# Counts of a GNN layer built two fifths at a time, heavy with light, and their place read from a four-word row

## The chip, the cores and the metric

The kernel runs on one core of a Trainium2 chip. The metric is the device time of one execution in microseconds (us), as the median of several runs. A change counts as faster or slower against the kernel before on the same chip.

## The reference, cut to what matters

A graph of 12500 nodes and 200000 edges goes through two SAGE layers, a last matrix and a layer norm. Edges come sorted by `dst`, and `dst` is drawn as 12500·u², so low nodes have far more edges than high ones.

```python
dst = (12500 * uniform(200000) ** 2.0).astype(int32)      # then sorted, src with it
def _sage_conv(x, src, dst, W_l, b_l, W_r):
    msgs = x[src]
    agg = segment_sum(msgs, dst, num_segments=N_NODES)
    deg = segment_sum(ones, dst, num_segments=N_NODES)
    mean = agg / maximum(deg, 1.0)[:, None]
    return mean @ W_l + b_l + x @ W_r
h = relu(_sage_conv(x, src, dst, W1_l, b1, W1_r))
h = relu(_sage_conv(h, src, dst, W2_l, b2, W2_r))
out = layernorm(x + (h @ W3 + b3))
```

## The kernel before

**Two ways to sum the messages.** The nodes are cut into 100 ranges of 125. The last 304 groups of 512 edges go the general way, in both layers: GpSimd (POOL in the profile) gathers rows of `x` by `src` into a ring of four groups (L420), VectorE (DVE) writes a one-hot matrix of `dst` (`mark_groups`, L929), TensorE (PE) multiplies the two (`pair`, L507), and DVE adds the product to `acc` (`add_product`, L907). The first 348 blocks of 128 edges belong to the five "hot" ranges, and go another way: a matrix of counts A[src, dst] is built once per hot range and multiplied with all rows of `x` ("dense steps", `dense_step`, L578), again in both layers.

**How counts are built.** A hot range has 25 chunks of five nodes. For each chunk DVE reads a row of a small table (`chunk_row`, L937: first block `hb` and the number of pairs of blocks `more`), marks each pair of blocks (`mark_blocks`, one L968 and two L971 a pair), PE multiplies the marks into the bank `psB` (`count_blocks`, L552), and DVE copies `psB` into `scratch` (`keep_counts`, L1012). The copy of one chunk stands just ahead of the marks of the next. Where it goes, and which store to DRAM must have landed first, DVE works out in registers from the number `kept` of chunks kept so far (L997 to L1009).

**Fifths.** Five chunks make a fifth, and `scratch` has two halves for a fifth each. SyncE (SP in the profile) stores a full half to DRAM (`store_part`, L363, 1250 KB), and the next fifth but one is written to the same half. Before, a fifth is built from its first chunk to its last, in the order third, fourth, fifth, first, second. The chunks of the first fifth of range 0 are the heavy ones, since its nodes have the most edges.

**The order of the work in layer 1.** All engines run the same written-out loop: stage 0 has 48 groups, and builds the counts of range 0. In each of the next four stages of 48 groups the counts of the next range are built while the last 40 groups also carry the 20 dense steps of the range before. A chunk is built after every second group. Then come the dense steps of the last range, and layer 2, in which no counts are built. SP's queue is in program order: for each dense step two loads of rows of `x` and one of counts (L326, L330, L349), which wait until the step two before has been used (L338), and between them the stores of the range under way: after steps 7, 11, 17 and 19 and at the end (`STORE`, L384).

```python
STORE = (7, 11, 17, 19)
turned = np.roll(np.arange(HW * CH).reshape(HW, CH), -2 * PART, axis=1).reshape(-1)   # order of chunks
```

Of the kernel before, what the change touches and what calls it, by code (L numbers as in the profile page):

```python
# [39 lines left out]
HW = 5  # L40
# [21 lines left out]
SW = 2 * (P + CJ)  # L62
STORE = (7, 11, 17, 19)
BANKS = 3
# [11 lines left out]
def hot_end(w):  # L76

    return 4 + STAGE * (w + 1) + STAGE


# [18 lines left out]
def constants():  # L99

    import numpy as np
    c = np.zeros((P, C_N), np.float32)
    c[:, C_ID:C_ID + P] = np.eye(P)
    c[0:WN, C_RES:C_RES + WN] = np.eye(WN)
    c[WN, C_RES:C_RES + WN] = 1
    c[:, C_WT:C_WT + NW] = WN * np.arange(NW)
    turned = np.roll(np.arange(HW * CH).reshape(HW, CH), -2 * PART, axis=1).reshape(-1)
    c[:, C_BS:] = CJ * turned
    order = np.array(ORDER)
    d = np.zeros((HW * CH, D_N), np.float32)  # L110
# [12 lines left out]
    b = np.arange(HB)  # L123
    d[:, D_RB:D_RB + HB] = HB - b
    d[:, D_RB + HB:] = b + 1
    w = np.append(order, 0).astype(np.int32).reshape(1, NW + 1) * RW
    k = np.arange(FN)
    n = np.concatenate([np.arange(CJ), k // (CD * SJ) * CJ + k % (CD * SJ)]).astype(np.int16)
    return c, d, w, n.reshape(1, CJ + FN)
# [10 lines left out]
def build(nc, x, src, dst, W1l, b1, W1r, W2l, b2, W2r, W3, b3, c_f, c_s, c_win, c_node, out):  # L140
# [5 lines left out]
    with ExitStack() as ctx:  # L146
# [35 lines left out]
        tab = tables[0:1, :]  # L182
        tabh = tables[32:33, 0:2 * (NH + NW) + 1]
        win = tables[64:65, 0:NW + 1]
# [100 lines left out]
        def _(sp):  # L285
# [29 lines left out]
            for q in range(2):  # L315
                sp.dma_start(xt[WN:WN + 1, q * D:(q + 1) * D], b3.rearrange("(a n) -> a n", a=1)).then_inc(s_w, 16)
            sp.dma_start(win, c_win).then_inc(s_w, 16)

# [39 lines left out]
            def store_part(w, f):  # L358

                n = w * PARTS + f  # L360
                sp.wait_ge(s_bank, credit[s_bank] + (n + 1) * PART)
                sp.wait_ge(s_kept, credit[s_kept] + 16 * n)
                sp.dma_start(a_dram[w * PARTS + (f + 2) % PARTS], scratch[:, n % 2 * JP * PW:(n % 2 + 1) * JP * PW]).then_inc(s_kept, 16)  # L363

# [61 lines left out]
        def _(pe):  # L426
# [40 lines left out]
            pe.wait_ge(s_ring1, 1)  # L467
            pe.wait_ge(s_w, 16 * 11)
            pe.wait_ge(s_set, 1)
# [13 lines left out]
            def turn_spans():  # L483

                pe.wait_ge(s_span, 1)
                for k, (a, n) in enumerate(((0, NH), (1, NH), (2, NW), (3, NW))):
                    pe.transpose(psT[0:1, k * 128:k * 128 + n], span[0:n, a:a + 1], ident[0:n, 0:n])
                pe.matmul(psT[0:1, 127:128], span[0:NW, 4:5], onec, start=True, stop=True).then_inc(s_spanT, 1)
                pe.wait_ge(s_tabh, 1)
                pe.load([wins], tabh[0:1, 2 * (NH + NW):2 * (NH + NW) + 1])  # L490

# [29 lines left out]

            def chunk_row():
                pe.load([more], tabh[0:1, bass.ds(pe.snap(at_row, min_val=1, max_val=2 * (NH + NW) - 1), 1)])
                pe.reg_add(at_row, at_row, 2)

# [56 lines left out]
            def fallback(l, q):  # L582

                W = RW if l == 0 else D
                pe.reg_mov(at_row, 2 * (NH + HW) + 1)
                end = pe.snap(wins, min_val=1, max_val=NW)
                if q == 0:
                    pe.reg_add(fin_x, fin_x, 32)
                pe.wait_ge(s_fall[q], pe.snap(fin_x, min_val=32, max_val=32 * STEPS))
                with pe.If(HW < end):  # L590
                    with pe.Fori(HW, end):
                        for h in range(2):
                            chunk_row()
# [160 lines left out]
        def _(v):  # L754
# [77 lines left out]
            v.wait_ge(s_set, 1)  # L832
            v.wait_ge(s_w, 16 * 11)
            v.wait_ge(s_k, 16)
# [10 lines left out]
            part, at_a = (v.alloc_register(f"v_{q}") for q in ("part", "at_a"))  # L845
            turned = v.alloc_register("v_turned")
            v.reg_mov(hot, 1)
            for r in (hadd, xdone, fdone, fb, kept):
                v.reg_mov(r, 0)
# [3 lines left out]
            def spans():  # L853

                v.wait_ge(s_limT, 1)
                th = tabh[0:1, 0:2 * (NH + NW)].rearrange("o (n c) -> o n c", c=2)
                for q, n in enumerate((NH, NW)):
# [25 lines left out]
                for q in range(2):  # L883
                    v.tensor_copy(th[:, 0:NH, q], psT[0:1, q * 128:q * 128 + NH])
                    v.tensor_copy(th[:, NH:, q], psT[0:1, (2 + q) * 128:(2 + q) * 128 + NW])
                link(v.tensor_copy(tabh[0:1, 2 * (NH + NW):], psT[0:1, 127:128]))
                v.sem_inc(s_tabh, 1)
                v.load([wins], tabh[0:1, 2 * (NH + NW):2 * (NH + NW) + 1])

# [46 lines left out]
            def chunk_row():  # L936
                v.load([hb, more], tabh[0:1, bass.ds(v.snap(at_row, min_val=0, max_val=2 * (NH + NW) - 2), 2)])  # L937
                v.reg_add(at_row, at_row, 2)
# [56 lines left out]
            def keep_counts():  # L995

                v.reg_alu(part, kept, 205, ALU.mult)  # L997
                v.reg_alu(part, part, 10, ALU.logical_shift_right)
                v.reg_alu(at_a, part, -PART, ALU.mult)
                v.reg_add(at_a, at_a, kept)  # L1000
                v.reg_alu(at_a, at_a, CD * SJ, ALU.mult)
                v.reg_add(kept, kept, 1)
                v.reg_alu(turned, part, 1, ALU.bitwise_and)
                v.reg_alu(turned, turned, JP * PW, ALU.mult)
                v.reg_add(at_a, at_a, turned)
                v.reg_alu(part, part, 16, ALU.mult)
                v.reg_add(part, part, credit[s_kept] - 16)
                at = v.snap(at_a, min_val=0, max_val=JP * PW + (PW - CD) * SJ)
                landed = v.snap(part, min_val=16, max_val=16 * HW * PARTS)  # L1009
# [26 lines left out]
            def fallback(l):  # L1036
                v.reg_mov(at_row, 2 * (NH + HW))
                end = v.snap(wins, min_val=1, max_val=NW)
# [6 lines left out]
                with v.If(HW < end):  # L1045
                    with v.Fori(HW, end) as w:
                        for h in range(2):
                            chunk_row()
                            chunk(FN, fbase[:, 0:1], CJ)
# [50 lines left out]
            def layer(l, dense):  # L1100
# [39 lines left out]
                if l == 0:  # L1140
# [7 lines left out]
                    with v.Fori(0, HW - 1) as w:  # L1148
                        chunk_row()
                        keep_counts()  # L1150
                        hot_chunk()
                        with v.Fori(0, STAGE // 4 - STEPS // 2):
                            four(builds=True)
                        with v.Fori(0, STEPS // 2):
                            four(builds=True, w=w)
                    keep_counts()
                    fallback_start()
# [32 lines left out]
        def _(act):  # L1190
# [26 lines left out]
            act.wait_ge(s_set, 1)  # L1217
            act.wait_ge(s_w, 16 * 11)
            give(act, s_tc, s_h, s_z, s_tc2, s_y, s_sd)
# [126 lines left out]
```

## Time and profile before

| | us |
|---|---|
| median of 3 runs (lowest, highest) | 3304.33 (3302.39, 3308.82) |
| the profiled execution: time, span | 3299.5, 3297.4 |
| busy in the span: PE, POOL, DVE, ACT | 2754.1, 2379.8, 1457.7, 497.5 |
| first and last copy of a chunk (L1012) start at | 72.4, 1374.4 |

The page gives each engine's busy time in the span from the first to the last instruction. A name like DVEq is an engine's queue: the register, branch and load instructions that are not counted as its work but take its time. "issue" is time in which an engine waited for nothing that the profile shows. The chain is the run of work that ended last, followed back from the end; what does not stand on it can grow a little at no cost.

### The profile page before, as it was taken

The numbers are of one execution on the slowest core, as the hardware profiler recorded it, in microseconds if no ns is written. First come the engines' busy times: TensorE is split into PE (matmuls) and PEld (weight loads), VectorE is DVE, ScalarE is ACT, GpSimd is POOL, SyncE is SP. The second block draws the span as 40 slices with busy tenths as digits, with TensorE's granted clock in tenths as the row PEclk, the third lists the DMA queues.
The fourth block names the chain that finished last, engine by engine and source line by source line (L and its number), as shares of the span: only waits on it lengthen the run. The fifth ranks groups of instructions, "written<-read, shape, count | busy, mean of one in ns | idle before, by whom it ended". The sixth has DMA issues, their size and how long they took to land.

```text
span 3297.4 us, 61445 instructions
## 1 busy us (share of the span) xinstructions
PE 2754.1 (84%) x13183; PEld 2294.5 (70%) x13184; DVE 1457.7 (44%) x3301; ACT 497.5 (15%) x1511; POOL 2379.8 (72%) x2439
## 2 busy tenths in 40 slices
PE   4788899899899899888866779878879879988876
PEld 3555687678678688677754567767768767767765
DVE  5676555555555555433323333333333333333332
ACT  2000110101111111111110112112112112212113
POOL 4765777677677677767747777777777777777775
PEclk7989999999999999999988889999999999999999
DMA  4443577577677777877655657757757757757743
GB/s 117 130 134 112 169 237 246 173 231 238 203 219 238 222 218 240 263 217 218 206 180 177 190 174 224 216 172 227 216 162 233 221 169 225 225 168 229 219 128 109
DMA packets 495816, 650.77 MB, mean 197 GB/s; under 512 B 184192, under 2 KB 414454, under 8 KB 492503
## 3 DMA queue, kind: packets, MB, share of 16 engines
q0 software_dynamic: 116736, 318.92, 32.6%
q1 hardware_dynamic: 298164, 253.95, 25.2%
q10 hardware_dynamic: 80800, 76.82, 7.7%
q14 instruction: 98, 0.78, 0.1%
q8 instruction: 18, 0.29, 0.0%
HBM read 579.07 MB, written 70.40 MB: 197 GB/s over the span
## 4 chain that ended last, share of the span: by engine, by line
PE 29%; POOL 24%; issue 18%; DVEq 14%; DMA 7%; DVE 7%; SPq 1%; ACT 1%; ACTq 0%; POOLq 0%; PEld 0%; PEldq 0%
POOL ring L420 24%; PE ps L507 16%; PE ps L578 5%; DMA ring<-z_rows,scol 4%; PE psY L622 3%; DVEq L917 2%; DVE oh L971 2%; PE psY L611 2%; DVEq L937 2%; DVE acc L907 1%; DMA counts<-scratch 1%; DVE oh L929 1%; PE psB L552 1%; DVEq L1067 1%; DVEq L914 1%
## 5 line engine op out<-in xcount | busy, mean ns | idle before, releaser
L507 PE MATMUL ps<-ring,oh 128*125 128x257 f32 (+1 forms) x6384 | 1586.9, 400 | 375.7 <-DMA ring<-z_rows,scol 203.6
L507 PEld LDWEIGHTS ps<-ring,oh 128*125 128x125 f32 x6384 | 1221.7, 196 | 649.5 <-issue 462.4
L420 POOL DMA_INDIRECT ring<-in_x,scol x1216 | 1193.4, 981 | 493.7 <-issue 349.8
L420 POOL DMA_INDIRECT ring<-z_rows,scol x1216 | 1185.8, 975 | 397.7 <-issue 355.5
L929 DVE SCALAR_TENSOR_TENSOR oh<-dcol,cf,iota 128x500 f32<-128x500 int16 x798 | 591.4, 741 | 609.9 <-issue 328.3
L907 DVE TENSOR_TENSOR acc<-ps,acc x802 | 338.8, 422 | 608.0 <-PE ps L507 415.4
L578 PE MATMUL ps<-scratch 128*125 128x257 f32 (+1 forms) x2000 | 481.2, 388 | 19.4 <-issue 13.4
L578 PEld LDWEIGHTS ps<-scratch 128*125 128x125 f32 x2000 | 456.1, 294 | 39.3 <-issue 21.5
L1268 ACT ACTIVATE work<-psT,b2c 128x125 f32<-128x125 f32 x200 | 62.0, 362 | 1196.2 <-PE psT L673 1196.2
L1232 ACT COPY work<-psY 125x256 f32<-125x256 f32 x100 | 37.2, 372 | 1306.1 <-PE psY L611 1306.1
L552 PE MATMUL psB<-oh 128*128 (+1 forms) x546 | 160.2, 391 | 81.7 <-DVE oh L971 80.7
L622 PEld LDWEIGHTS psY<-work,w 128*128 128x128 f32 x1600 | 200.6, 197 | 7.4 <-issue 1.1
L622 PE MATMUL psY<-work,w 128*128 128x125 f32 x1600 | 199.8, 280 | 0.7 <-issue 0.7
L971 DVE TENSOR_SCALAR oh<-iota,cf,key 128x500 int16 (+1 forms) x546 | 199.4, 407 | 0.0
L552 PEld LDWEIGHTS psB<-oh 128*128 (+1 forms) x546 | 50.0, 97 | 173.8 <-issue 145.0
L1012 DVE COPY scratch<-psB 128x500 f32 x125 | 84.9, 679 | 114.0 <-issue 104.2
L611 PE MATMUL psY<-w,hT 128*125 128x256 f32 x400 | 113.5, 409 | 17.7 <-issue 16.0
L669 PE MATMUL psT<-hT,w 128*128 x800 | 121.8, 275 | 0.1
L669 PEld LDWEIGHTS psT<-hT,w 128*128 128x128 f32 x800 | 113.0, 192 | 6.4 <-issue 0.5
L968 DVE TENSOR_TENSOR oh<-iota,key 128x256 int16 (+1 forms) x273 | 114.4, 419 | 6.9 <-PE psB L552 4.5
L655 PE MATMUL psY<-w,work 128*125 128x256 f32 x400 | 106.5, 389 | 3.4 <-ACT work L1268 2.6
L611 PEld LDWEIGHTS psY<-w,hT 128*125 128x125 f32 x400 | 73.2, 196 | 49.7 <-issue 36.7
(120 smaller groups left out, 1100.2 us busy)
## 6 DMA issues: line engine op xcount, KB each, us to landing
scratch<-counts SPq DMA_DIRECT2D x200, 312.5 KB
scratch<-in_x SPq DMA_DIRECT2D x114, 512.0 KB, 4.2
scratch<-z_rows SPq DMA_DIRECT2D x114, 512.0 KB, 4.0
counts<-scratch SPq DMA_DIRECT2D x25, 1250.0 KB
work<-in_x ACTq DMA_DIRECT2D x200, 125.0 KB
ring<-in_x,scol POOLq DMA_INDIRECT x1216
ring<-z_rows,scol POOLq DMA_INDIRECT x1216
scratch<-in_x SPq DMA_DIRECT2D x114, 128.0 KB, 5.2
```

The lines of the kernel that those rows point to most:

```text
L420: pool.indirect_dma_start(ring[:, slot, b, 0:D], None, rows_dram, bass.IndirectOffsetOnAxis(scol[:, n - C0:n - C0 + 1], 0)).then_inc(rows[ ...
L507: mm = pe.matmul(psA[0:WN, bass.ds(bank, W)], oh[:, R if later else slot, b, :], ring[:, slot, b, 0:W], start=(b == 0), stop=(b == nb - 1))
L552: mm = pe.matmul(psB[:, 0:n], oh1[:, bass.ds(at, P)], oh1[:, bass.ds(at + P, n)], start=first and b == 0, stop=True, skip_group_check=True)
L578: mm = pe.matmul(psD[0:WN, 0:W], lin_a[:, q, :, :, k].rearrange("p f n -> p (f n)"), lin_x[:, q, k, 0:W], start=(q == 0 and k == 0), stop= ...
L611: mm = pe.matmul(psZ[0:WN, 0:D], hT[:, k * WN:(k + 1) * WN], w2[:, k, 0:D], start=(k == 0), stop=(k == 1))
L622: mm = pe.matmul(psH[:, m * WN:(m + 1) * WN], w1[:, a, k, m * P:(m + 1) * P], tT[:, 2 * a + k, :], start=(a == 0 and k == 0), stop=(a == 1 ...
L655: pe.matmul(at, tT[:, k, :], w3[:, k, :], start=(k == 0), stop=False)
L669: pe.matmul(psT[:, m * WN:(m + 1) * WN], w2[:, k, D + m * P:D + (m + 1) * P], hT[:, bass.ds(q + k * WN, WN)], start=(k == 0), stop=False)
L907: v.tensor_tensor(at, psA[0:WN, bass.ds(v.snap(par, min_val=0, max_val=(BANKS - 1) * 512), W)], at, ALU.add).then_inc(s_ad[l], 1)
L929: v.scalar_tensor_tensor(out=ohf[:, at:at + nb * WN].rearrange("p (b n) -> p b n", n=WN), in0=dcol[:, bass.ds(blk, nb)].unsqueeze(2).to_br ...
L968: v.tensor_tensor(s[:, :, 0:P], iota[:, 0:P].unsqueeze(1).to_broadcast([P, 2, P]), key[:, 0, bass.ds(at, 2)].unsqueeze(2).to_broadcast([P, ...
L971: ins = v.tensor_scalar(s[:, b, P:P + n], iota[:, table:table + n], base, key[:, 1, bass.ds(at + b, 1)], ALU.add, ALU.is_equal)
```

## The change

The order of chunks is now written in a table `TURNS`. The fifths are taken in the order second, third, first, fifth, fourth (`PORD`). The chunks of the second and third are built in turn, then those of the first (heavy) and fifth, then the fourth alone. A chunk's table row has four words in place of two: the third is the place in `scratch` where the chunk before goes, loaded by SP from a constant at the start. `keep_counts` works out the store to wait for from `kept`, which is set to 0 at each range. Stores stand after dense steps 6, 7, 16 and 17 and at the end, and wait for 9, 10, 19, 20 and 25 kept chunks.

```diff
-STORE = (7, 11, 17, 19)
+STORE = (6, 7, 16, 17)
+PORD = (1, 2, 0, 4, 3)
+DONE = (9, 10, 19, 20, 25)
+TW = 4 * (HW * CH + 1)
+TURNS = [(2 * m + q, i) for m in range(2) for i in range(PART) for q in range(2)] + [(4, i) for i in range(PART)]
...
-    turned = np.roll(np.arange(HW * CH).reshape(HW, CH), -2 * PART, axis=1).reshape(-1)
+    turned = np.array([w * CH + PORD[f] * PART + i for w in range(HW) for f, i in TURNS])
...
+    rows = np.zeros((HW * CH + 1, 4), np.int32)
+    rows[1:, 2] = [(w * PARTS + f) % 2 * JP * PW + i * CD * SJ for w in range(HW) for f, i in TURNS]
...
-            sp.dma_start(win, c_win).then_inc(s_w, 16)
+            sp.dma_start(win, c_win[:, 0:NW + 1]).then_inc(s_w, 16)
+            sp.dma_start(tabh[:, 0:TW], c_win[:, NW + 1:]).then_inc(s_w, 16)
...
-                sp.wait_ge(s_bank, credit[s_bank] + (n + 1) * PART)
+                sp.wait_ge(s_bank, credit[s_bank] + w * CH + DONE[f])
                 sp.wait_ge(s_kept, credit[s_kept] + 16 * n)
-                sp.dma_start(a_dram[w * PARTS + (f + 2) % PARTS], scratch[...]).then_inc(s_kept, 16)
+                sp.dma_start(a_dram[w * PARTS + PORD[f]], scratch[...]).then_inc(s_kept, 16)
...
             def chunk_row():
-                v.load([hb, more], tabh[0:1, bass.ds(v.snap(at_row, min_val=0, max_val=2 * (NH + NW) - 2), 2)])
-                v.reg_add(at_row, at_row, 2)
+                v.load([hb, more, at_a, spare], tabh[0:1, bass.ds(v.snap(at_row, min_val=0, max_val=TW - 4), 4)])
+                v.reg_add(at_row, at_row, 4)
...
             def keep_counts():
                 v.reg_alu(part, kept, 205, ALU.mult)
-                v.reg_alu(part, part, 10, ALU.logical_shift_right)
-                v.reg_alu(at_a, part, -PART, ALU.mult)
-                v.reg_add(at_a, at_a, kept)
-                v.reg_alu(at_a, at_a, CD * SJ, ALU.mult)
+                v.reg_alu(part, part, 11, ALU.logical_shift_right)
+                v.reg_alu(part, part, 32, ALU.mult)
+                v.reg_alu(side, kept, 1, ALU.bitwise_and)
+                v.reg_alu(side, side, 16, ALU.mult)
+                v.reg_add(part, part, side)
+                v.reg_add(part, part, kept_w)
                 v.reg_add(kept, kept, 1)
-                v.reg_alu(turned, part, 1, ALU.bitwise_and)
-                v.reg_alu(turned, turned, JP * PW, ALU.mult)
-                v.reg_add(at_a, at_a, turned)
-                v.reg_alu(part, part, 16, ALU.mult)
-                v.reg_add(part, part, credit[s_kept] - 16)
...
                     with v.Fori(0, HW - 1) as w:
                         chunk_row()
                         keep_counts()
+                        v.reg_mov(kept, 0)
+                        v.reg_add(kept_w, kept_w, 16 * PARTS)
                         hot_chunk()
...
+                    chunk_row()
                     keep_counts()
```

On DVE's queue the place is between a group's sum (L907, L918 after the change) and the copy of the counts. Before:

```order
L937 ISA
L937 TENSOR_LOAD tables
L938 ISA
L907 ISA
L907 TENSOR_TENSOR acc<-ps,acc 125x257
L911 ISA
L914 ISA
L1003 REGISTER_ALU
L1004 ISA
L993 REGISTER_ALU
L1012 ISA
L1012 COPY scratch<-psB 128x20x25
```

After:

```order
L948 ISA
L948 TENSOR_LOAD tables
L949 ISA
L918 ISA
L918 TENSOR_TENSOR acc<-ps,acc 125x257
L922 ISA
L925 ISA
L1015 REGISTER_ALU
L1016 ISA
L1024 ISA
L1024 COPY scratch<-psB 128x20x25
```

One register instruction between the sum and the copy is gone, and the load (the same instruction) now brings four words.

On SP's queue the place is the first two stores of a range among the loads of the dense steps of the range before (each step is counts, rows, last rows). Before, from step 7 to step 11:

```order
43 L349 DMA scratch<-counts 128x5x125
44 L326 DMA scratch<-in_x 128x4x256
45 L330 DMA scratch<-in_x 128x256
46 L363 DMA counts<-scratch 128x2500
...
56 L349 DMA scratch<-counts 128x5x125
57 L326 DMA scratch<-in_x 128x4x256
58 L330 DMA scratch<-in_x 128x256
59 L363 DMA counts<-scratch 128x2500
```

After, from step 6 to step 7:

```order
41 L358 DMA scratch<-counts 128x5x125
42 L335 DMA scratch<-in_x 128x4x256
43 L339 DMA scratch<-in_x 128x256
44 L372 DMA counts<-scratch 128x2500
45 L358 DMA scratch<-counts 128x5x125
46 L335 DMA scratch<-in_x 128x4x256
47 L339 DMA scratch<-in_x 128x256
48 L372 DMA counts<-scratch 128x2500
```

The two stores stood four steps apart and stand one step apart. Which chunk is built when does not show in either queue, since the loop body is the same and a chunk's number of passes is read from the table.

## Rows read from the trace of the kernel before

**Rows 1.** Busy us by stretch: PE, PEld, DVE, ACT, POOL; PEclk, DMA share, GB/s

```profile
60.00:217.00 157.00, 126.90 (x561) 92.24 (x562) 100.68 (x243) 12.22 (x34) 116.07 (x118) 0.91 0.45 132
217.00:363.00 146.00, 115.84 (x491) 75.59 (x491) 101.72 (x258) 12.32 (x35) 83.37 (x84) 0.89 0.41 125
363.00:1400.00 1037.00, 937.98 (x4737) 780.77 (x4735) 582.19 (x1376) 112.70 (x320) 762.52 (x780) 0.98 0.73 224
```

**Rows 2.** Waits in stage 0, 60 to 363 us: total, times, longest

```profile
POOL ring L420 <- PE ps L507: 47.6, 18, 13.1
PE psB L552 <- DVE oh L971: 40.9, 75, 3.6
```

**Rows 3.** Waits in stages 1 to 4, 363 to 1400 us

```profile
POOL ring L420 <- PE ps L507: 49.3, 40, 8.0
...
DVE scratch L1012 <- DMA counts<-scratch: 9.7, 9, 1.7
PE ps L507 <- DMA ring<-in_x,scol: 2.3, 2, 1.7
```

**Rows 4.** The chain by line, 60 to 363 us and 363 to 1400 us

```profile
by line: issue 22.3%; PE ps L507 13.2%; DVE oh L971 7.8%; PE psY L622 4.4%; PE psB L552 4.0%; DVEq L937 3.9%; DVEq L917 3.4%; DVE oh L968 3.2%; DVEq L971 3.1%; DVE acc L907 3.1%; PE psY L611 2.6%; DVEq L914 2.3%; DVEq L981 2.1%; DVEq L983 2
...
by line: issue 17.0%; PE ps L507 16.8%; PE ps L578 7.2%; PE psY L622 5.7%; DVEq L917 5.4%; DMA counts<-scratch 4.2%; DVEq L937 3.8%; PE psY L611 3.3%; DVE oh L971 2.9%; DVE acc L907 2.6%; PE psB L552 2.2%; DVE oh L929 1.9%; DVEq L914 1.9%; 
```

**Rows 5.** L968 (one a pair of blocks) from copy to copy; PEclk, DMA share, GB/s

```profile
136.00:144.50 8.50, 1.26 (x3) 1.00 0.38 108
217.00:240.70 23.70, 6.77 (x16) 0.67 0.31 104
...
287.50:297.20 9.70, 1.68 (x4) 1.00 0.39 113
```

**Rows 6.** The chain between a sum and the copy that follows it

```profile
882.33 0.23 DVEq L914
...
882.68 0.20 DVEq L1004
...
882.92 0.04 DVEq L993
...
883.01 0.02 DVEq L1011
```

**Rows 7.** First and last pieces of L1004 and of L937's load on the chain

```profile
61.56 0.54 DVEq L937
...
81.10 0.20 DVEq L1004
...
1367.18 0.55 DVEq L937
...
1373.95 0.20 DVEq L1004
```

**Rows 8.** Loads from the table in 363 to 1400 us: ns min/median/max

```profile
L937 DVEq TENSOR_LOAD <-tables x98: 532/547/1623, 368.3 to 1367.2; - x98
...
L917 DVEq TENSOR_LOAD <-tables x97: 608/830/3093, 367.6 to 1390.6; - x97
```

**Rows 9.** The copies that a store held up, in order of time

```profile
570.66 0.68 DVE L1012 COPY scratch<-psB 128x500 f32 x1 [1.69 <-DMA counts<-scratch]
...
725.95 0.68 DVE L1012 COPY scratch<-psB 128x500 f32 x1 [1.42 <-DMA counts<-scratch]
...
828.86 0.68 DVE L1012 COPY scratch<-psB 128x500 f32 x1 [1.00 <-DMA counts<-scratch]
...
1338.16 0.68 DVE L1012 COPY scratch<-psB 128x500 f32 x1 [1.75 <-DMA counts<-scratch]
```

**Rows 10.** Two pieces of the chain: SP's issue at the start, a store

```profile
20.75 0.31 SPq L321
...
716.69 9.05 DMA counts<-scratch
```

**Rows 11.** The same columns as rows 1, while a store is under way

```profile
496.00:505.00 9.00, 7.42 (x33) 5.66 (x32) 4.16 (x10) 0.00 (x0) 6.87 (x8) 1.00 0.99 334
```

More of the change, by code:

```diff
@@ L125, in constants @@
     d[:, D_RB + HB:] = b + 1
-    w = np.append(order, 0).astype(np.int32).reshape(1, NW + 1) * RW
+    rows = np.zeros((HW * CH + 1, 4), np.int32)
+    rows[1:, 2] = [(w * PARTS + f) % 2 * JP * PW + i * CD * SJ for w in range(HW) for f, i in TURNS]
+    w = np.concatenate([order * RW, [0], rows.reshape(-1)]).astype(np.int32).reshape(1, NW + 1 + TW)
     k = np.arange(FN)
@@ L182, in build @@
         tab = tables[0:1, :]
-        tabh = tables[32:33, 0:2 * (NH + NW) + 1]
+        tabh = tables[32:33, 0:TW + 2 * NW + 1]
         win = tables[64:65, 0:NW + 1]
@@ L360, in store_part @@
                 n = w * PARTS + f
-                sp.wait_ge(s_bank, credit[s_bank] + (n + 1) * PART)
+                sp.wait_ge(s_bank, credit[s_bank] + w * CH + DONE[f])
                 sp.wait_ge(s_kept, credit[s_kept] + 16 * n)
-                sp.dma_start(a_dram[w * PARTS + (f + 2) % PARTS], scratch[:, n % 2 * JP * PW:(n % 2 + 1) * JP * PW]).then_inc(s_kept, 16)
+                sp.dma_start(a_dram[w * PARTS + PORD[f]], scratch[:, n % 2 * JP * PW:(n % 2 + 1) * JP * PW]).then_inc(s_kept, 16)
             def fallback(rows_dram, t0, t1):
@@ L467, in _ @@
             pe.wait_ge(s_ring1, 1)
-            pe.wait_ge(s_w, 16 * 11)
+            pe.wait_ge(s_w, 16 * 12)
             pe.wait_ge(s_set, 1)
@@ L489, in turn_spans @@
                 pe.wait_ge(s_tabh, 1)
-                pe.load([wins], tabh[0:1, 2 * (NH + NW):2 * (NH + NW) + 1])
+                pe.load([wins], tabh[0:1, TW + 2 * NW:TW + 2 * NW + 1])
             def next_bank():
@@ L520, in row_of, with chunk_row @@
                 return (front[0:4], back[4:8], front[4:8], back[0:4])[i]
-            def chunk_row():
-                pe.load([more], tabh[0:1, bass.ds(pe.snap(at_row, min_val=1, max_val=2 * (NH + NW) - 1), 1)])
-                pe.reg_add(at_row, at_row, 2)
+            def chunk_row(words=4):
+                pe.load([more], tabh[0:1, bass.ds(pe.snap(at_row, min_val=1, max_val=TW + 2 * NW - 1), 1)])
+                pe.reg_add(at_row, at_row, words)
             def group(l, i, nb, builds=False):
@@ L584, in fallback @@
                 W = RW if l == 0 else D
-                pe.reg_mov(at_row, 2 * (NH + HW) + 1)
+                pe.reg_mov(at_row, TW + 2 * HW + 1)
                 end = pe.snap(wins, min_val=1, max_val=NW)
@@ L592, in fallback @@
                         for h in range(2):
-                            chunk_row()
+                            chunk_row(2)
                             chunk(FN)
@@ L832, in _ @@
             v.wait_ge(s_set, 1)
-            v.wait_ge(s_w, 16 * 11)
+            v.wait_ge(s_w, 16 * 12)
             v.wait_ge(s_k, 16)
@@ L845, in _ @@
             part, at_a = (v.alloc_register(f"v_{q}") for q in ("part", "at_a"))
-            turned = v.alloc_register("v_turned")
+            turned, kept_w, spare, side = (v.alloc_register(f"v_{q}") for q in ("turned", "kept_w", "spare", "side"))
             v.reg_mov(hot, 1)
+            v.reg_mov(kept_w, credit[s_kept] - 16)
             for r in (hadd, xdone, fdone, fb, kept):
@@ L855, in spans @@
                 v.wait_ge(s_limT, 1)
-                th = tabh[0:1, 0:2 * (NH + NW)].rearrange("o (n c) -> o n c", c=2)
+                th = tabh[0:1, 0:TW].rearrange("o (n c) -> o n c", c=4)
+                tw = tabh[0:1, TW:TW + 2 * NW].rearrange("o (n c) -> o n c", c=2)
                 for q, n in enumerate((NH, NW)):
@@ L884, in spans @@
                     v.tensor_copy(th[:, 0:NH, q], psT[0:1, q * 128:q * 128 + NH])
-                    v.tensor_copy(th[:, NH:, q], psT[0:1, (2 + q) * 128:(2 + q) * 128 + NW])
-                link(v.tensor_copy(tabh[0:1, 2 * (NH + NW):], psT[0:1, 127:128]))
+                    v.tensor_copy(tw[:, :, q], psT[0:1, (2 + q) * 128:(2 + q) * 128 + NW])
+                link(v.tensor_copy(tabh[0:1, TW + 2 * NW:], psT[0:1, 127:128]))
                 v.sem_inc(s_tabh, 1)
-                v.load([wins], tabh[0:1, 2 * (NH + NW):2 * (NH + NW) + 1])
+                v.load([wins], tabh[0:1, TW + 2 * NW:TW + 2 * NW + 1])
             def next_bank():
@@ L936, in chunk_row, with range_row @@
             def chunk_row():
-                v.load([hb, more], tabh[0:1, bass.ds(v.snap(at_row, min_val=0, max_val=2 * (NH + NW) - 2), 2)])
+                v.load([hb, more, at_a, spare], tabh[0:1, bass.ds(v.snap(at_row, min_val=0, max_val=TW - 4), 4)])
+                v.reg_add(at_row, at_row, 4)
+            def range_row():
+                v.load([hb, more], tabh[0:1, bass.ds(v.snap(at_row, min_val=TW, max_val=TW + 2 * NW - 2), 2)])
                 v.reg_add(at_row, at_row, 2)
@@ L997, in keep_counts @@
                 v.reg_alu(part, kept, 205, ALU.mult)
-                v.reg_alu(part, part, 10, ALU.logical_shift_right)
-                v.reg_alu(at_a, part, -PART, ALU.mult)
-                v.reg_add(at_a, at_a, kept)
-                v.reg_alu(at_a, at_a, CD * SJ, ALU.mult)
-                v.reg_add(kept, kept, 1)
-                v.reg_alu(turned, part, 1, ALU.bitwise_and)
-                v.reg_alu(turned, turned, JP * PW, ALU.mult)
-                v.reg_add(at_a, at_a, turned)
-                v.reg_alu(part, part, 16, ALU.mult)
-                v.reg_add(part, part, credit[s_kept] - 16)
+                v.reg_alu(part, part, 11, ALU.logical_shift_right)
[4 more added lines that the diff above has]
+                v.reg_add(part, part, kept_w)
+                v.reg_add(kept, kept, 1)
                 at = v.snap(at_a, min_val=0, max_val=JP * PW + (PW - CD) * SJ)
-                landed = v.snap(part, min_val=16, max_val=16 * HW * PARTS)
+                landed = v.snap(part, min_val=16, max_val=16 * HW * PARTS + 32)
                 counted()
@@ L1036, in fallback @@
             def fallback(l):
-                v.reg_mov(at_row, 2 * (NH + HW))
+                v.reg_mov(at_row, TW + 2 * HW)
                 end = v.snap(wins, min_val=1, max_val=NW)
@@ L1047, in fallback @@
                         for h in range(2):
-                            chunk_row()
+                            range_row()
                             chunk(FN, fbase[:, 0:1], CJ)
@@ L1217, in _ @@
             act.wait_ge(s_set, 1)
-            act.wait_ge(s_w, 16 * 11)
+            act.wait_ge(s_w, 16 * 12)
             give(act, s_tc, s_h, s_z, s_tc2, s_y, s_sd)
```

## The prediction

> **What bounds the kernel now.** I read busy time by stretch first, then the waits in the stretches that the change touches, then the chain, then single instructions. Counts are built from 72 to 1374 us only, so nothing after that changes but by a shift. In stage 0 PE is busy 81 and 79% of the two parts, DVE 64 and 70%, POOL 74 and 57% [rows 1]. No engine is full, and POOL falls back in the second part, which has the heavy fifth. The waits say who is late. POOL waits 47.6 us for PE to free ring slots, while PE waits 40.9 us for DVE's marks [rows 2]; PE waits for no gathered row in that stretch. So stage 0 is a serial walk from DVE to PE and back, with POOL ahead of both. In stages 1 to 4 PE is busy 90%, POOL waits 49.3 us for it, and PE waits 2.3 us for gathered rows [rows 3]. The chain there runs over PE's matmuls and over DVE's queue: the loads L917 and L937 hold 5.4 and 3.8% [rows 4]. A shorter DVE queue is thus worth something in both, a faster gather is not.
>
> **Part 1, the order of chunks.** It removes no work. What would it be worth that a heavy chunk is followed by a light one? With two groups and no finished range beside it, a chunk of 3 pairs takes 8.5 us from copy to copy, one of 4 pairs 9.7, one of 16 pairs 23.7 [rows 5]: (23.7 - 8.5) / 13 = 1.17 us a pair, and 1.2 for the fourth. The granted clock was 0.67 in the stretch of 16 pairs and 1.00 in the two others [rows 5], so that slope already holds what the clock costs. Cost by pair is a sum, and a sum doesn't care for order, unless the ring runs empty in light stretches before (then a heavy chunk beside them would be hidden). It never does [rows 2]. I put 0 us, and 4 us either way for the clock falling in other places (3 or 4% of the 146 us of the heavy part [rows 1]): a chunk of many pairs has PE wait on DVE wherever it stands.
>
> **Part 2, register work between sum and copy.** The chain goes from L914 by L1004 and L993 to L1011 [rows 6]. The eleven register operations of keep_counts become eight. L993, a whole instruction, is gone: from its start at 882.92 to the next at 883.01 are 0.09 us. The other two operations go out of fused instructions, of which L1004 takes 0.20. So at least 0.09 us, and at most three whole steps, 0.27; I take 0.13, the step and L993's own 0.04 once more. L1004 stands on the chain 81 times of 125 (first and last in [rows 7]); in the other 44 PE's matmuls hide it. 81 × 0.13 = 10.5 us saved (7.3 to 22).
>
> **Part 3, four words in a load in place of two.** The trace has no load of four words on DVE. Two words take 532 ns at least and 547 in the median, eight take 608 and 830 [rows 8]. By the least, two words more cost (608 - 532) / 3 = 25 ns, by the medians (830 - 547) / 3 = 94 ns. By the chain: L937 holds 3.9% of 303 us and 3.8% of 1037, together 51.2 us, of which I count 75 loads with 48.8 us, 0.65 each; L917 holds 3.4 and 5.4%, 66.3 us in 60 loads, 1.11 each [rows 4, 7]: a third of the difference is 152 ns. Long ones occur in both (1.6 and 3.1 us at most). I take the medians, between the ends: 75 × 0.094 = 7.1 us lost (1.9 to 11.4).
>
> A rule of the Trainium skill speaks against this edit. Its page Runtime: NRT & Kernel Launch, section Instruction fetch mechanics, gives a register load from HBM some 200 ns a register "even for bulk". An estimate by that page: two words cost 0.4 us a row, 75 rows 30 us, and the sum below would be a loss of 18 us. The trace here reads SBUF, and its least times (532 ns for two words, 608 for eight) disagree with 200 ns a word.
>
> **Part 4, the stores.** Before, four copies waited for a store, 1.69, 1.42, 1.00 and 1.75 us [rows 9], where some 0.7 is register work that comes anyway (882.33 to 883.01 in [rows 6]; the 9.7 us of [rows 3] count that, and five more rows of it). The excess is 5.86 - 4 × 0.7 = 3.1 us. Each is the first chunk of a fifth whose half was stored one chunk ago: a store takes 9.05 us from issue [rows 10], a chunk some 10.4 (1037 us by 100). After, SP's store is free to go as soon as the ninth, tenth, nineteenth or twentieth chunk is kept, and the first chunk that needs its half is two chunks later: 21 us against 9. The waits go: -3.1 us. What the stores may hold up: on SP they queue ahead of the loads for steps 7 and 8. The kept chunk that a store waits for comes half a step before that load could go, and the load has a further step of 20 us. On the DMA engines one store drives their share from a mean of 0.73 to 0.99 and the rate from 224 to 334 GB/s [rows 1, 11]. Two stores in 21 us ask for 224 + 2 × 1250 KB / 21 us, about 346 GB/s against 334: an overflow of 1 us a pair, eight pairs, hidden by a ring that PE does not wait for. Nothing, and 8 us if that cover were gone.
>
> **Part 5, small things.** One DMA more on SP at the start, where the chain runs from issue to issue: 0.3 us, like L321 [rows 10]. One row more is read after the last range, 0.6 us by [rows 8], and register moves at four ranges, 0.2. Together +1.1 us.
>
> **The sum.** -10.5 + 7.1 - 3.1 + 1.1 = -5.4 us. The profiled execution took 3299.5 us (span 3297.4 and 2.1 around it) and would take 3294.1. The median of the runs is 4.8 us above it, so I forecast 3299 for the median of after: less than before by 0.16%. About 0.2%, 6.6 us, is what a measurement of this kernel can tell from no change.
>
> **The rivals.**
> - *The load is cheap and the register work dearer than I take.* For it: the least times, and that four words are nearer two than eight. -10.5 × 1.1 + 1.9 - 3.1 + 1.1 = -11.7: 3293. Chance 0.21.
> - *The order pays: the heavy fifth was lost time for POOL, and now is not.* For it: POOL is at 57% there against 74. At the first part's rate (157 us for 118 gathers) its 84 gathers would take 112 us and not 146 [rows 1]. If 25 of these 34 us came back: 3275. Against: the chain has no POOL in its largest lines [rows 4], and PE never waits for rows there. Chance 0.08.
> - *It is a wash.* The load costs what the chain's mean says (11.4), and half of part 2 falls to the second longest path, PE's: -5.3 + 11.4 - 1.6 + 1.1 = +5.6, or 3310 at worst, near 3306 as likely. For it: DVE's 8-word loads in stages 1 to 4 have a median far above their least time. Chance 0.18.
> - *Slower: words cost by the piece while the DMA engines are full.* The longest 8-word load is 2.5 us above the least, 0.41 us a word. At half of that, 0.2 us a word, the rows lose 75 × 0.4 = 30 us, the sum is +18: 3322. It decides from 0.127 us a word, where 75 × 2 × 0.127 = 19.1 us outweigh the 12.5 saved by 6.6. Against: 0.076 is the highest mean slope here. Chance 0.09. The rule of the Trainium skill named above (Runtime: NRT & Kernel Launch) is this case.
>
> **How the numbers follow.** Forecast 0.44, with 3294 to 3304 as its own range. Faster by over 0.2% means below 3297.7: the first two rivals (0.29) and a quarter of the forecast, 0.40. Slower means above 3310.9: the last rival and the tail of the wash, 0.11. Within 0.2%: 0.49. The range from 3287 to 3312 leaves out the order's gain and the slower rival.
>
> **What the profile of after would show.** Right: L1004's successor followed at once by the copy's wait, sum to copy some 0.1 us shorter; the four-word load with a median near 0.6 us and a mean below 0.75; no copy of counts held by a store; POOL's waits for PE in stage 0 again near 48 us, in smaller pieces after 190 us, and stage 0 as long as before. Wrong: stage 0 shorter by over 6 us (then the order pays); the four-word load's median above 0.8 us; PE waiting for the ring or dense steps for rows after step 6 or 16, which would be the paired stores.

## The result and the profile after

| | before | after |
|---|---|---|
| median of the runs | 3303.36 us (3301.62 to 3308.82, 4 runs) | 3268.48 us (3266.92 to 3272.49, 4 runs) |
| ratio, 95% interval | | 0.9896 [0.9882, 0.991] |
| profiled execution | 3299.5 us, span 3297.4 | 3267.8 us, span 3265.6 |

The change made the kernel faster by 1.04%, 35 us in the median and 32 in the profiled execution. I had forecast 3299 and a range from 3287 to 3312, so the time lies 30 us below the one and 19 below the other.

The loads come first, since the prediction hung on their price. These are the loads of the table of chunks in stages 1 to 4 (ns, least, median, most), with the answer to L937 of [rows 8]:

```profile
L948 DVEq TENSOR_LOAD <-tables x99: 341/355/1726, 362.9 to 1345.4; - x99
```

And the eight-word load beside it, which was L917:

```profile
L928 DVEq TENSOR_LOAD <-tables x99: 605/825/2670, 370.1 to 1395.7; - x99
```

Four words take 355 ns where two took 547, while the eight-word load, which the diff doesn't touch, stayed within 5 ns. I had put a price on the wider load, and it is 0.19 us shorter.

The trace of before already held a second thing that sets a load's length, and I missed it. The three small tables lie in partitions 0 (eight words, L917), 32 (the chunk rows, L937) and 64 (the next range's place, L1067) of one tile. Sorted by which table VectorE's load before had read, the 111 eight-word loads behind a load from partition 0 or 32 have a median of 609 ns, and the 194 behind one from partition 64 have 821 (least 812), though microseconds pass between the two loads. The one-word load takes 317 to 328 ns three times out of the four that it follows itself (731 once), and 539 in the median of 196 behind one of the others (all worked out from the loads in order of time). Two stretches of before, the first behind partition 64, the second with the one-word load behind itself:

```profile
L917 DVEq TENSOR_LOAD <-tables x2: 818/818/819, 268.6 to 280.9; - x2
...
L1067 DVEq TENSOR_LOAD <-tables x2: 317/322/327, 3279.5 to 3284.0; - x2
```

Going between partition 64 and the other two thus costs some 0.21 us a load; why is not known.

Next the chain between a sum and the copy that follows it, as in [rows 6] (start us, us, what):

```profile
881.38 0.11 DVEq L925
...
881.52 0.05 DVEq L1015
...
881.60 0.22 DVEq L1016
...
881.87 0.02 DVEq L1023
...
881.94 0.06 DVEq L1024
882.00 0.05 issue
882.04 0.11 DVE scratch L1024
```

The whole instruction L993 is gone, and L1016 stands for L1004. Over all 125 chunks the start of the copy follows the start of the sum after 963 ns in the median, and after 1193 before (worked out from the starts of the two instructions of each chunk): 0.23 us less, where I took 0.13. That lies between the ends that I gave, 0.09 and 0.27. Half of it is not where I looked: by the medians over the chunks L914 took 233 ns and L925 takes 120, L993 and its gap took 0.09 us, and L1016 is even longer than L1004, 217 ns to 198.

The time by stretch, with the columns of [rows 1]:

```profile
60.00:217.00 157.00, 125.69 (x499) 81.18 (x498) 109.08 (x277) 9.20 (x26) 98.48 (x102) 0.84 0.38 113
217.00:363.00 146.00, 122.84 (x576) 90.61 (x575) 98.05 (x237) 15.40 (x44) 102.79 (x104) 0.94 0.51 154
363.00:1400.00 1037.00, 946.19 (x4809) 795.89 (x4808) 590.42 (x1392) 116.44 (x330) 782.95 (x795) 0.98 0.74 228
```

The heavy fifth now lies in the first part of stage 0. There the clock granted was 0.84, against 0.91 in the same stretch before, and in the second part 0.94 against 0.89: the order moved the low clock, and did not remove it. The chunk with most pairs, alone:

```profile
170.50:199.40 28.90, 24.52 (x76) 11.57 (x75) 21.80 (x58) 1.76 (x5) 8.11 (x10) 0.65 0.30 102
```

It has the same 16 pairs and as low a clock (0.65) as the stretch in [rows 5] (0.67); its 28.9 us, for 23.7 there, hold ten gathers to eight and three sums to two.

The waits of stage 0 (60 to 363 us), as in [rows 2]:

```profile
POOL ring L429 <- PE ps L516: 44.7, 17, 18.4
...
PE psB L561 <- DVE oh L986: 36.2, 71, 3.5
```

And those of stages 1 to 4 (363 to 1400 us), as in [rows 3]:

```profile
PE ps L516 <- DMA ring<-in_x,scol: 25.5, 12, 5.2
POOL ring L429 <- PE ps L516: 24.8, 42, 4.8
...
DVE scratch L1024 <- DMA counts<-scratch: 4.3, 8, 0.5
```

In stage 0 nothing much moved: 3 us less on the one side, 5 on the other. In the later stages POOL's waits for PE halved and PE's waits for gathered rows grew from 2.3 to 25.5 us. A faster consumer empties the ring more often. No copy waits for a store any more; what is left of that wait, 0.5 us at most, is the register work that comes anyway.

The chain by line in the same two stretches says it more clearly, as in [rows 4]:

```profile
by line: issue 21.2%; PE ps L516 17.6%; DVE oh L986 7.6%; PE psB L561 5.1%; PE psY L631 4.3%; DVEq L928 3.2%; DVE oh L983 3.1%; DVE acc L918 3.0%; DVEq L986 3.0%; PE psY L620 2.7%; DVEq L948 2.5%; DVE oh L940 2.1%; DVEq L996 2.0%; DVEq L998
...
by line: PE ps L516 19.1%; POOL ring L429 17.8%; issue 16.6%; PE ps L587 7.2%; PE psY L631 5.2%; DMA ring<-in_x,scol 4.8%; DVEq L928 3.1%; PE psY L620 3.0%; PE psB L561 2.6%; DVE oh L986 1.4%; DVE acc L918 1.4%; DVEq L948 1.4%; PE psT L646 
```

The load's share fell from 3.9 to 2.5% and from 3.8 to 1.4%. POOL's issue of gathers, which stood nowhere on the chain of before in stages 1 to 4, holds 17.8% of them. It is not that a gather became dearer. The gathers of that stretch, after:

```profile
L429 POOL DMA_INDIRECT ring<-in_x,scol x795: 941/947/1454, 362.5 to 1399.9; - x199
```

Before, 780 of them had a median of 946 ns. The changed kernel comes to the same gather sooner, and POOL now sets part of the pace.

The stores have a part in this too. The chain's 4.8% of gathers in flight are these seven pieces; before, it had one such piece, the last line:

```profile
439.15 6.50 DMA ring<-in_x,scol
794.33 7.16 DMA ring<-in_x,scol
954.10 7.80 DMA ring<-in_x,scol
1047.74 7.18 DMA ring<-in_x,scol
1194.12 6.54 DMA ring<-in_x,scol
1296.41 6.86 DMA ring<-in_x,scol
1347.55 7.35 DMA ring<-in_x,scol
...
1330.73 7.42 DMA ring<-in_x,scol
```

SP issued a store 0.1 to 4.1 us before each of the seven (at 435.5, 792.6, 952.7, 1046.3, 1190.5, 1292.4 and 1347.4 us), and of PE's 25.5 us of waits for rows 18.6, in 8 waits of 12, end while a store is under way or within 1.5 us of its landing. Six of the seven stores belong to a pair, but one of these is the second of its pair and the seventh stands alone, so the pairing is not shown to be the cause. In the 190 us after the issues of a store in stages 1 to 4 (9.5 us each) PE was busy 84% before and 82% after, some 3 us more of idle time, and an estimate of what the pairs can have cost.

Where the 32 us of the profiled executions came from, stage by stage, from a stage's first copy of counts to the next one's: 290.9, 257.6, 262.3 and 254.6 us before, 284.1, 251.5, 253.5 and 249.7 after, and 236.6 against 234.2 to the last copy. That is 6.8, 6.1, 8.8, 4.9 and 2.4 us less, 29 in all. The first copy came 1.3 us later, and some 4 us were gained after the last, where the two kernels run the same code. Stage 0, alone to hold the heavy fifth, gained no more than the next two did on average. The last two gained least, and there POOL's pieces on the chain are densest: I count 63 of about 1 us from 1000 to 1200 us, and 11 from 360 to 600.

### The profile page after: what moved, and what is told of

The parts are those of the page before. It is cut to its first block, busy times and chain, and to the rows that moved or that the text cites. A ratio compares the mean times of both kernels' runs of the same rounds, so it can differ in the third digit from the quotient of the medians.

```text
span 3265.6 us, 61269 instructions
## 1 busy us (share of the span) xinstructions
PE 2761.8 (85%) x13183; PEld 2310.7 (71%) x13184; DVE 1460.5 (45%) x3301; ACT 498.3 (15%) x1511; POOL 2381.1 (73%) x2439
## 4 chain that ended last, share of the span: by engine, by line
PE 32%; POOL 28%; issue 17%; DVEq 9%; DMA 7%; DVE 5%; ACT 1%; SPq 1%; ACTq 0%; PEldq 0%; PEld 0%; POOLq 0%
POOL ring L429 28%; PE ps L516 19%; PE ps L587 5%; DMA ring<-z_rows,scol 4%; PE psY L631 2%; DMA ring<-in_x,scol 2%; DVEq L928 2%; PE psY L620 1%; PE psB L561 1%; DVE oh L986 1%; DVE acc L918 1%; PE psY L664 1%; DVE oh L940 1%; PE psT L678 1%; DVEq L948 1%
## 5 line engine op out<-in xcount | busy, mean ns | idle before, releaser
L516 PE MATMUL ps<-ring,oh 128*125 128x257 f32 (+1 forms) x6384 | 1606.2, 404 | 370.5 <-DMA ring<-z_rows,scol 185.7
L516 PEld LDWEIGHTS ps<-ring,oh 128*125 128x125 f32 x6384 | 1237.4, 199 | 650.0 <-issue 455.6
L918 DVE TENSOR_TENSOR acc<-ps,acc x802 | 338.5, 422 | 589.7 <-PE ps L516 404.7
```

What stands on the lines that cost most here:

```text
L516: mm = pe.matmul(psA[0:WN, bass.ds(bank, W)], oh[:, R if later else slot, b, :], ring[:, slot, b, 0:W], start=(b == 0), stop=(b == nb - 1))
L918: v.tensor_tensor(at, psA[0:WN, bass.ds(v.snap(par, min_val=0, max_val=(BANKS - 1) * 512), W)], at, ALU.add).then_inc(s_ad[l], 1)
```

## The experiments

Three questions were open. Is the shorter load due to its width, or to the sixteen bytes that a row now takes? What do the load, the register work and the order bring each? And what would a microsecond on VectorE's queue be worth from here? The twelve kernels ran in three groups of four, each on one chip with the kernel before beside them. On these three chips every kernel took some 600 to 670 us longer than on the first (before: 3905, 3970 and 3960 us), so all ratios are to before on the same chip, and us are compared inside a group alone. Their traces hold some loads of a few ns, too short to be whole, so the medians are read there and not the least. And no wait of PE for gathered rows in layer 1 stands in these traces, so they cannot tell what the stores cost on the first chip.

**load4: the load alone.** Old order, old stores, old register work; the row has four words and all four are loaded, two of them unused. The table is laid out as in the changed kernel, with its DMA more at the start.

```diff
-                v.load([hb, more], tabh[... 2)])
+                v.load([hb, more, side, spare], tabh[... 4)])
-                v.reg_add(at_row, at_row, 2)
+                v.reg_add(at_row, at_row, 4)
```

> The kernel before, with one thing of the change: a chunk's row has four words and the load on DVE's queue brings all four (two are not used); order, stores and register work are the old ones. Theory A (the load itself got shorter, 547 to 350 ns in the median, and that is near half of the gain): the load at about 350 ns, some 75 of them on the chain, 75 x 0.2 = 15 us less than before, about 3288. Theory B (the gain is the order of chunks and the stores): 3303, as before, whatever the load takes. My prediction's own term would have been 3310.

> As load4. It took 353 ns for the load in the median and came out 0.28% below the kernel before. If a load's 0.2 us comes back in full on the 75 rows of the chain: 0.45% or 15 us below before. If other paths take its place: 0.25 to 0.3%, 9 us.

Measured: 0.9972 [0.9946, 0.9998], and in the second group 0.9941 [0.9922, 0.9961], which is 11 and 21 us less. The load in the second:

```profile
L948 DVEq TENSOR_LOAD <-tables x125: 3/354/1111, 60.9 to 1703.0; - x125
```

**load2_stride4: the same rows of four words, two of them loaded.**

```diff
-                v.load([hb, more, side, spare], tabh[... 4)])
+                v.load([hb, more], tabh[... 2)])
```

> As load4, but the load brings only two words of the four-word row, so that the row's address steps by 16 bytes as after the change. If the width of the load is what matters: 547 ns in the median and 3303, as before. If the step or alignment of the rows is: 350 ns and about 3288, as load4.

Measured: 1.0011 [0.9986, 1.0037]. The two-word load is as long as ever, though it too now starts at a multiple of 16 bytes:

```profile
L948 DVEq TENSOR_LOAD <-tables x125: 3/533/1353, 61.3 to 1685.2; - x125
```

So the row's place gives nothing by itself. What is short is the load of four words.

**shift2: the changed kernel, its table two words further on.** The four-word load then starts at an odd multiple of 8 bytes.

```diff
-        tabh = tables[32:33, 0:TW + 2 * NW + 1]
+        tabh = tables[32:33, 2:TW + 2 * NW + 3]
```

> The changed kernel with the table of chunk rows two words further on in its partition, so that each four-word load starts at an odd multiple of 8 bytes instead of a multiple of 16; nothing else differs. Theory A (the place of the first word decides): the load takes some 570 ns as the lower half of the four-word loads at every place in wide_next did, against 350 aligned, so 125 chunks pay 0.2 us each: up to 25 us more on VectorE's queue, of which about half lands in the time, ratio to the changed kernel 1.003 to 1.006. Theory B (the number of words alone decides): load still 350 ns and the same time within 0.1%.

> The changed kernel once more, as the bar for the three kernels sent with it: the row's load at a median near 353 ns, 0.96 us from the start of a chunk's sum to the start of its copy, ratio to before 0.990 to 0.994.

Measured: after_third, the changed kernel itself, 0.9911 [0.9881, 0.994], 3928 us; shift2 1.0026 [1.0002, 1.0049], 3969 us. The load, in after_third and then in shift2:

```profile
L948 DVEq TENSOR_LOAD <-tables x126: 3/353/1073, 60.9 to 1701.6; - x126
```

```profile
L948 DVEq TENSOR_LOAD <-tables x126: 15/973/3533, 62.1 to 1748.0; - x126
```

Theory B falls. Theory A named the place rightly and the price wrongly: not 570 ns but 973 (the 570 came from loads of wide_next that were themselves at a multiple of 16 bytes, see there). Eight bytes of offset cost 0.62 us a load, and turn a kernel that is 0.9% faster than before into one that is 0.3% slower. It also gives the exchange rate, what a microsecond on VectorE's queue is worth in the time: 0.62 × 125 = 78 us on the queue, 41 us of the time, so 0.53.

**no_turns: the load and the register work, without the order and the stores.** The changed kernel with the fifths in turn as before, eight register operations, one with a factor of 0.

```diff
-STORE = (6, 7, 16, 17)
-PORD = (1, 2, 0, 4, 3)
-DONE = (9, 10, 19, 20, 25)
+STORE = (7, 11, 17, 19)
+PORD = (2, 3, 4, 0, 1)
+DONE = (5, 10, 15, 20, 25)
-TURNS = [(2 * m + q, i) for m in range(2) ...
+TURNS = [(f, i) for f in range(PARTS) for i in range(PART)]
```

> The changed kernel with the old order of fifths and chunks (none built in turn) and the old places of the stores; the place still comes with the four-word row, and the eight register operations stay eight (one multiplies by 0). Theory A (load and register work, 0.2 + 0.23 us a chunk, 80 of them on the chain): nearly all of the gain stays, 3270 to 3275. Theory B (order and stores): the gain is gone, 3290 or more.

> As no_turns. Against after_again it shows what order and stores are worth together. Theory A (load and register work are the gain): within 5 us of after_again, of which 3 are the four waits for a store. Theory C, formed after the last runs (no_turns kept 25 us, wait_from_row 61): order and stores are worth a third or more of the gain, 10 to 15 us slower than after_again.

> The changed kernel once more, as the common ground for the three beside it, since the chip of the last four took 3905 us for the kernel before. Ratio to the kernel before 0.9896, as measured first, if this chip is like the first.

Measured: no_turns 0.9936 [0.9912, 0.9959], 15 us below load4 beside it; no_turns_again 0.9915 [0.9894, 0.9937], 13 us below load4_again; after_again 0.9921 [0.9893, 0.9949], 8 us above no_turns_again, inside both intervals. The register work is worth 13 to 15 us there, and order and stores together nothing that can be told. From the first copy to that of the next range no_turns_again took 378.7 us and after_again 382.3: no gain from the order shows in stage 0, where it should have. The stores' term is seen, if small, in the copies held by a store in the whole program, first in no_turns_again, then in after_again:

```profile
DVE scratch L1024 <- DMA counts<-scratch: 6.3, 2, 3.6
```

```profile
DVE scratch L1024 <- DMA counts<-scratch: 1.1, 2, 0.5
```

**wait_from_row: no register work at all before the copy.** The row's fourth word, unused in the changed kernel, holds the store to wait for.

```diff
+    rows[1:, 3] = [32 + 16 * (w * PARTS + f - 1) for w in range(HW) for f, i in TURNS]
...
-                v.reg_alu(part, kept, 205, ALU.mult)
-                ... (eight operations in all, and two at each range)
-                landed = v.snap(part, min_val=16, max_val=16 * HW * PARTS + 32)
+                landed = v.snap(spare, min_val=16, max_val=16 * HW * PARTS)
```

> The changed kernel with the store to wait for read from the row's fourth word too, so that no register work of keep_counts is left between the sum and the copy. If DVE's queue still bounds: 0.3 us less a chunk, sum to copy 0.65 us, some 10 to 20 us less than the changed kernel, about 3253. If POOL's issue of gathers (18% of the chain in 363 to 1400 us after the change) has become the bound: under 5 us less, 3265 to 3268.

> The kernel whose row also holds the store to wait for, so that no register work stands before the copy, on the same chip as the changed kernel. Theory: 0.29 us less per chunk between sum and copy (0.67 instead of 0.96 us), and 81 or so chunks on the chain give 10 to 25 us: ratio to before 0.984 to 0.989, below after_third by 0.3 to 0.7%. Rival: VectorE has left the chain by now, since GpSimd's queue of gathers and TensorE's wait for rows have grown in the changed kernel; then it equals after_third within 0.2%.

Measured: 0.9845 [0.9806, 0.9885] and 0.9862 [0.9838, 0.9886], 24 us below after_third beside it. From sum to copy are 0.67 us in both (0.97 in after_third). It beats both kernels on the chips where it ran. The rival, that VectorE had left the chain, falls on those chips; that PE waited less for marks and POOL less for PE fits. The waits from 70 to 1700 us in after_third, then in wait_from_row_again:

```profile
POOL ring L429 <- PE ps L516: 331.1, 85, 22.9
...
PE psB L561 <- DVE oh L986: 98.9, 76, 7.9
```

```profile
POOL ring L430 <- PE ps L517: 296.2, 80, 20.9
...
PE psB L562 <- DVE oh L987: 90.8, 72, 7.8
```

But on these chips POOL still waits more than 290 us for PE, and in the first chip's profile 70 (44.7 and 24.8). What is left to gain from VectorE's queue on a chip like the first wasn't measured, and is likely to be less.

**wide_next and wide_aligned: the same trick for the next range's place.** On top of wait_from_row, the one-word load after each finished range takes four words; in wide_aligned the table has four words to a range as well.

```diff
-                v.load([at_tile], win[0:1, bass.ds(i + 1, 1)])
+                v.load([at_tile, part, side, turned], win[0:1, bass.ds(i + 1, 4)])        # wide_next
+                v.load([at_tile, part, side, turned], win[0:1, bass.ds((i + 1) * 4, 4)])  # wide_aligned
```

> wait_from_row with one more thing: the place of the next range's sums is read with a load of four words in place of one (three are not used), on DVE's queue, 200 times. By the law that the width decides (four words 350 ns, two 535, one 535), each load is 0.19 us shorter, and those on the chain bring 10 to 20 us: ratio to before 0.980 to 0.984. If the law holds for the chunk's table alone (its own partition), the load stays near 535 ns and the ratio is that of wait_from_row.

> The kernel before this one, in which the load of the next range's place (84 times, one word, 535 ns) takes four words from a table with four words to a place, so that it starts at a multiple of 16 bytes. Theory A (place and width decide together): 350 ns a load, 0.18 us less for each of some 84 loads, up to 15 us less on VectorE's queue, perhaps 3 to 8 us of the time. Theory B (wide loads are short only where chunks are built): about 535 to 1200 ns as in wide_next, and no gain or 10 us more.

Measured: wide_next 0.9879 [0.9854, 0.9904], wide_aligned 0.987 [0.9847, 0.9893], the latter 3 us above wait_from_row_again. The load, whose one word took 532 ns, in wide_next and then in wide_aligned:

```profile
L1072 DVEq TENSOR_LOAD <-tables x200: 3/1198/3176, 96.0 to 3893.8; - x100
```

```profile
L1072 DVEq TENSOR_LOAD <-tables x200: 3/569/2319, 98.6 to 3885.1; - x100
```

A misplaced four-word load is dear here too. By place, wide_next's loads have medians of 1204, 1201 and 1202 ns at the three places that are no multiple of 16 bytes, and 569 at the fourth. An aligned one is not short here, 569 ns, so the price in theory A of wide_aligned was wrong; but its rival, that wide loads are short only where chunks are built, is not the reason. What lengthens the load is which partition VectorE's load before had read. These loads read partition 64, and all but four follow one of partition 0 or 32. Two of the four, in wide_aligned:

```profile
L1072 DVEq TENSOR_LOAD <-tables x2: 351/351/351, 3880.5 to 3885.1; - x2
```

That is the chunk load's price; of the other two one took 354 ns and one 684. The other way round, the four chunk loads of the changed kernel that follow a read of partition 64 took 557 to 659 ns. The time between the loads does not matter: 33 chunk loads that start more than 2 us after a load from partition 0 ended have a median of 355 ns, like the 60 that follow within 0.3 us (350). So place, width and the partition read before set the length together. No run moved the table out of partition 64.

## Why the prediction was wrong

**What bounds the kernel** was right: a walk between DVE and PE, where DVE's queue counts and the gather doesn't. In after it is right no longer for stages 1 to 4.

**Part 3 is the step that failed.** "By the least, two words more cost (608 - 532) / 3 = 25 ns, by the medians (830 - 547) / 3 = 94 ns" draws a line through two points, and the load is not on it: at a multiple of 16 bytes four words take 355 ns, less than two. A gain was never among the ends of that price, though nothing in the trace excluded one. My rows were of two widths, and the place of the first word was in none of my terms. The slope by the medians was wrong by its own rows too: 62 of the 97 eight-word loads of stages 1 to 4 stood behind a read of partition 64 and the two-word loads nearly never; like for like it is (623 - 547) / 3 = 25 ns. In place of +7.1 us, my own 75 rows on the chain give 75 × (547 - 355) ns = 14.4 us saved. load4 measured 11 and 21 us, on chips that take 3900 us. The rule of the Trainium skill's page Runtime: NRT & Kernel Launch (section Instruction fetch mechanics), 200 ns a register, would have had the load 0.4 us longer; it fell by 0.19, and the slower rival with it. Away from a multiple of 16 bytes the measured step is near that rule: 973 ns in shift2 against 547 for two words, 0.43 us for two words more, and in before 0.22 from one word (328) to two.

**Part 2** was the right mechanism with too small a size: 0.23 us a chunk and not 0.13, so 81 × 0.23 = 18.6 us in place of 10.5. I charged the fused instructions 0.04 us for losing operations, and looked for it in L1004; L914 alone gave back 0.11. no_turns against load4 measured 15 and 13 us, there with 0.18 us less a chunk (1194 to 1014 ns). The 81 places are those of before's chain; in after L1016 stands on the chain 51 times, so the last part of this saving went to the next path, POOL's.

**Part 1** stands as far as it was measured: 0 us for the order, by the ring that never ran empty in stage 0, with the two kernels of the second group, which differ in order and stores, 8 us apart on the side of a loss and within what they can tell. On the first chip the order was not measured apart. The rival "the order pays" named nearly the time that came (3275), and nothing shows its mechanism: stage 0 gained 6.8 us, as much as stages that have no heavy fifth.

**Part 4** was right in kind: no copy is held any more, 3.1 us by its own rows. Its cover, a ring that PE does not wait for, is gone: PE waited 25.5 us for rows, 18.6 of them beside a store, and seven gathers in flight beside stores stand on the chain. The part had put up to 8 us on that case; PE's busy share beside stores, 84 and 82%, lets the cost be some 3 us, and no run measured it. **Part 5** was not measured apart.

With the two measured sizes the sum is -18.6 - 14.4 - 3.1 + 1.1 = -35.0 us, where the medians differ by 34.9 and the profiled executions by 31.7. So close a fit is partly luck. It counts the places of before's chain, of which L1016 keeps 51 of 81 in after, and the exchange rate of shift2, 0.53, on (0.23 + 0.19) × 125 = 52.5 us gives 28, and 31 with the stores.

**What I said the profile would show.** Right: sum to copy shorter, no copy held, POOL's waits in stage 0 near 48 us. Wrong: the load's median near 0.6 us, and stage 0 as long as before; by my own sign, 6 us less in stage 0 was to mean that the order pays, and it doesn't mean that, since stage 1 lost nearly as much. One more sign of being wrong came true, PE waiting for the ring beside the stores after steps 6 and 16, at 440, 700, 802 and 962 us among others.

## What to carry to other kernels

When a price is missing from a trace, an interpolation between two widths is a guess about the law as well as the number: let its range reach below zero, and look at the address too, not at the width alone. A table row that is read in one four-word load should start at a multiple of 16 bytes; two words of offset cost more here than the whole change brought. Before a median is used as a price, sort its rows by what came before them: here that splits one median of 830 ns into 623 and 896. Some 390 loads of the kernel stand behind a load across the border of partition 64, at 0.21 us each; whether the small table in partition 0 or 32 would win that back is the next thing to try. And words that such a load brings along can replace register arithmetic on a critical queue, 0.23 us a time here and 0.29 more with the fourth word in use, until another engine takes over the chain.

## What the runs showed of the hardware

- A load of registers from SBUF on VectorE's queue took, in the median and behind a load from the same side (partition 0 or 32, or partition 64): 328 ns for one word, 533 to 546 for two, whether or not they start at a multiple of 16 bytes (load2_stride4, before), 353 for four and 609 for eight at a multiple of 16, and 973 for four at an odd multiple of 8 (shift2). By these numbers words come one at a time for some 0.21 us each, but four together at a multiple of 16 bytes; that this is the mechanism was not tested.
- Behind a load from the other side each was some 0.2 us longer: 539 ns for one word, 773 for two (three loads), 571 for four (four loads), 821 for eight, and 1201 to 1204 for four away from a multiple of 16 bytes (wide_next), where 973 and 0.2 us make 1.18.
- TensorE's one-word load of the same table took 305 ns in the median in both kernels. TensorE reads no table in partition 64, and VectorE's 328 ns is the number to set beside it.
- The same kernels took 3905 to 3970 us on three chips and 3303 on the first. Their granted clock was 0.88 against 0.95, and much of the rest stands in the profile as idle time of VectorE and others that no semaphore ends; its cause was not sought.
